# Two scatters in flight instead of four in the routing stage of a four-block kernel

## The chip, the cores and the metric

The kernel runs as one program on one core of one Trainium2 chip. The metric is the device time of one execution in microseconds (us), from the first to the last instruction plus what lies around them; less is better. The kernel before was timed three times.

## What is computed

The reference is four blocks in a row on 8 sequences of 256 tokens of width 256 (2048 tokens), each a residual of a layer norm: attention with 16 heads, a mixture of experts (MoE), a state-space block with 32 heads, and a feed-forward network. The change touches the second:

```
logits = flat @ router_w                       # 2048 tokens, 64 experts
_, topk_idx = top_k(logits + router_bias, 4)
g = silu(einsum('nd,edf->nef', flat, wg));  u = einsum('nd,edf->nef', flat, wu)
routed = einsum('ne,nef,efd->nd', comb, g * u, wd)
shared = two shared experts of hidden width 256 for every token
x = x + layernorm(routed + shared)
```

Only the four chosen experts of a token have a weight in `comb`, so the kernel computes only those.

## The kernel before

One core holds all 2048 tokens as 16 tiles of 128 tokens (`NT = 16`), handled in four chunks of four tiles (`NCH`, `TPC`). The program is a row of stages; each ends in a barrier of all engines. Two stages matter here.

**The routing stage** (`stage_route`). TensorE turns the normalised rows and scores each chunk, VectorE picks the four best experts of each token and works out, for each token and choice, a row number in a table `slots_in` in device memory (128 tiles of 128 rows, each tile owned by one expert). Row numbers of one chunk are ready when `find_slots(g)` has run (the last instruction of it is L1220, semaphore `slots_ready`). VectorE's order is written out by hand: `find_slots(0)`, statistics of x for chunk 2 and 3, `find_slots(1)`, then, when chunks 2 and 3 have been scored, `find_slots(2)`, a step of the shared experts, `find_slots(3)`, and the other shared-expert steps.

GpSimd carries the rows out. For each of the 16 tiles and each of the four choices it issues one indirect DMA (L957, a scatter): the 128 rows of 1 KB of a tile of `rows` go to the 128 row numbers in `slots`. That makes 64 scatters of 128 KB, 16 for each chunk. They use `IN_FLIGHT` semaphores in turn, and scatter n waits until scatter n - `IN_FLIGHT` has landed:

```
if n == BEFORE_ROWS:                                          # 6
    for late in range(EARLY_NORMS, NCH): deviations(OF_X, late)
if n >= IN_FLIGHT:
    pool.wait_ge(scattered[n % IN_FLIGHT], n // IN_FLIGHT * 16)
nc.gpsimd.indirect_dma_start(out=xs[:, :], ...                # L957
    ).then_inc(scattered[n % IN_FLIGHT], 16)
```

A DMA raises its semaphore by 16 when all of it has landed. After the sixth scatter GpSimd computes the deviations and shifts of x for the chunks 2 and 3 (L446, L447). ScalarE needs them to fill `rows` of these chunks (L452), TensorE turns what ScalarE filled (L971), and the scores, the slots and the scatters of these chunks hang on that.

The queue of SyncE issues four loads of expert weights, waits for the semaphores of all scatters, and issues the loads of the first three quads of rows from `slots_in` (`load_quad`, L851).

**The stage behind it** (`stage_slots`) starts after the barrier (L926 is where the routing stage's block closes). TensorE turns quad g (L1359) when its load has landed.

Beside the scatters, TensorE, ScalarE and VectorE compute the shared experts of chunks 0 and 1 (L1032, L1042 on TensorE; L1111, L1115 on ScalarE; L1236, L1240 on VectorE), which ends this stage.

Nothing else waits for single scatters: the semaphores `scattered` are read by GpSimd's own waits and by SyncE alone.

Of the kernel before, what the change touches and what calls it, by code (L numbers as in the profile page):

```python
# [820 lines left out]
COPIES = 3 * QUAD  # L821
DEEP = 3
AHEAD = 4
IN_FLIGHT = 4
WEXP = D + P
U32 = mybir.dt.uint32
I32 = mybir.dt.int32
# [30 lines left out]
def stage_route(chip, x, rows, norms, xh, xl, y, ident, xs, t, ahead, router, ins):  # L858
# [10 lines left out]
    with ExitStack() as ctx:  # L869
# [44 lines left out]
        owner_found, owner_turned, owner_out = (chip.sem(n) for n in ("owner_found", "owner_turned", "owner_out"))  # L914
        slots_ready, scattered = chip.sem("slots_ready"), [chip.kept_sem("scattered") for _ in range(IN_FLIGHT)]
        gate_done, up_done, silu_done = chip.sem("gate_done"), chip.sem("up_done"), chip.sem("silu_done")
# [9 lines left out]
        with nc.Block() as block:  # L926
            @block.sync
            def _(sp):
                for q in range(AHEAD):
                    load_experts(sp, ahead, ins, q, ahead["w_loaded"][q])  # L930
                for done in scattered:
                    sp.wait_ge(done, NT * TOPK // IN_FLIGHT * 16)
                for g in range(DEEP):
# [3 lines left out]
            def _(pool):  # L937
# [3 lines left out]
                def deviations(kind, g):  # L941
                    pool.wait_ge(var_ready, normed(kind, g))
                    spread(nc, link, norms, kind, range(g * TPC, (g + 1) * TPC)).then_inc(rstd_ready, 1)
# [3 lines left out]
                for g in range(NCH):  # L947
                    pool.wait_ge(slots_ready, g + 1)
                    for i in range(g * TPC, (g + 1) * TPC):
                        for k in range(TOPK):  # L950
                            n = i * TOPK + k
                            if n == BEFORE_ROWS:
                                for late in range(EARLY_NORMS, NCH):
                                    deviations(OF_X, late)
                            if n >= IN_FLIGHT:
                                pool.wait_ge(scattered[n % IN_FLIGHT], n // IN_FLIGHT * 16)
                            nc.gpsimd.indirect_dma_start(  # L957
                                out=xs[:, :], out_offset=bass.IndirectOffsetOnAxis(slots[:, i, k:k + 1], 0),
                                in_=rows[:, i, :], in_offset=None).then_inc(scattered[n % IN_FLIGHT], 16)

# [1907 lines left out]
```

## Time and profile before

| | us |
|---|---|
| median of three runs | 1359.48 |
| lowest, highest | 1359.06, 1362.21 |
| the profiled execution, own time | 1354.88 |
| its span, first to last instruction | 1353.1 |
| TensorE busy in it | 1159.4 (86%) |
| VectorE busy | 855.6 (63%) |
| ScalarE busy | 620.5 (46%) |
| GpSimd busy | 362.0 (27%) |
| routing stage, first scatter to its barrier | 258.65 to 372.6 |

The profile is of one execution. The profiled execution's own time lies 4.6 us under the median of the runs, and 1.8 us over its span. Times in the rows are us from the start of the span, durations us unless marked ns. POOL is GpSimd, PE TensorE's matmuls, PEld its weight loads, DVE VectorE, ACT ScalarE, SPq and POOLq the queues of SyncE and GpSimd. A GpSimd row of a scatter is the time in which its descriptors are made, and the transfer comes behind it.

### The profile page before, as it was taken

To read this page: it belongs to the slowest core of one execution; us is meant where nothing else is said; L and a number is where in the kernel's file an instruction comes from. 1 tells how busy PE (TensorE), PEld (TensorE's weight loads), DVE (VectorE), ACT (ScalarE), POOL (GpSimd) and SP (SyncE) were. 2 spreads that over 40 slices of the span, in tenths; PEclk is the share of its full clock that TensorE was granted. 3 is DMA by queue.
4 is the path that set the end of the run, shared out by engine and by line. 5 is a ranking of instruction groups with operands and counts; after the bars stand their busy time and mean duration, and the time that the engine had idled before them with its cause. 6 is when DMAs were issued, how large, how long until landed. Compare 5 with 4: busy or idle time off the path is not lost. (4 is left out here: it accounts for less than half of the span.)

```text
span 1353.1 us, 25314 instructions
## 1 busy us (share of the span) xinstructions
PE 1159.4 (86%) x9088; PEld 966.7 (71%) x9088; DVE 855.6 (63%) x2162; ACT 620.5 (46%) x1420; POOL 362.0 (27%) x460
## 2 busy tenths in 40 slices
PE   6669997347599988677789999999999999999895
PEld 5546775345498977555558888888888888888775
DVE  6467896727566656587365666666666666664474
ACT  5434554112144432467644554554454445553564
POOL 3321231375401437583042014002400240000110
PEclk9779998558899998887899999999999999999898
DMA  6648874121399764253243233223342332221001
GB/s 176 180 120 221 231 204 169 58 101 65 107 360 401 271 246 126 79 183 135 86 119 102 79 102 118 78 79 105 115 140 84 108 107 82 83 86 67 1 17 47
DMA packets 77961, 177.21 MB, mean 131 GB/s; under 512 B 12614, under 2 KB 26182, under 8 KB 75270
## 3 DMA queue, kind: packets, MB, share of 16 engines
q1 hardware_dynamic: 71564, 158.54, 36.2%
q0 software_dynamic: 6272, 17.05, 4.2%
q8 instruction: 73, 1.20, 0.4%
q14 instruction: 52, 0.43, 0.1%
HBM read 114.26 MB, written 61.08 MB: 130 GB/s over the span
## 5 line engine op out<-in xcount | busy, mean ns | idle before, releaser
L2300 ACT ACTIVATE decay<-masked,negcum 128x128 f32<-128x128 f32 x512 | 164.0, 391 | 240.7 <-issue 156.1
L2216 PE MATMUL joint<-xh,w_high 128*128 128x512 f32 x512 | 211.7, 413 | 1.7 <-POOL wl L2157 1.7
L2216 PE MATMUL joint<-xh,wl 128*128 128x512 f32 x512 | 200.6, 392 | 0.0
L2405 DVE COPY cT<-joint 128x512 f32<-128x512 f32 x128 | 88.4, 691 | 176.3 <-PE joint L2216 176.3
L2216 PE MATMUL joint<-xl,w_high 128*128 128x512 f32 x512 | 199.7, 390 | 0.0
L2227 PEld LDWEIGHTS pcb<-cT,bT 128*128 128x128 f32 x1024 | 134.5, 191 | 10.6
L2227 PE MATMUL pcb<-cT,bT 128*128 128x128 f32 x1024 | 135.3, 275 | 0.0
L2154 POOL TENSOR_TENSOR w_high<-w_in,none 128x512 fp32r<-128x512 f32 x32 | 34.6, 1083 | 319.5 <-DMA w_in<-in_w_bc 319.4
L2216 PEld LDWEIGHTS joint<-xh,w_high 128*128 128x128 f32 x512 | 96.5, 188 | 22.5 <-issue 4.8
L2216 PEld LDWEIGHTS joint<-xh,wl 128*128 128x128 f32 x512 | 96.1, 188 | 21.1
L2216 PEld LDWEIGHTS joint<-xl,w_high 128*128 128x128 f32 x512 | 96.6, 189 | 15.3
L2364 DVE TENSOR_TENSOR mixT<-pcb,decay 128x512 f32<-128x512 f32 x128 | 88.5, 692 | 26.2 <-PE pcb L2227 25.9
L2354 DVE TENSOR_TENSOR masked<-cumrow,mask 128x512 f32<-128x512 f32 x128 | 92.2, 721 | 0.0
L697 ACT ACTIVATE probT<-pst 128x384 f32<-128x384 f32 x128 | 60.2, 490 | 65.2 <-PE pst L628 61.8
L2319 ACT ACTIVATE bT<-joint 128x512 f32<-128x512 f32 x128 | 74.3, 581 | 26.3 <-PE joint L2216 26.3
L957 POOL DMA_INDIRECT slots_in<-rows,slots x64 | 65.4, 1023 | 50.5 <-DVE slots L1220 31.8
L1580 POOL DMA_INDIRECT back<-slots_out,slots x64 | 70.2, 1098 | 28.4 <-issue 27.3
L1448 DVE TENSOR_TENSOR rows<-gate,pgu 64x512 f32<-64x512 f32 x64 | 44.2, 691 | 31.2 <-ACT gate L1423 30.8
L1326 POOL COPY copies<-weights 128x384 f32 x64 | 32.4, 507 | 106.3 <-issue 84.7
L2373 DVE TENSOR_TENSOR cS<-cT,grown 128x256 f32<-128x256 f32 x128 | 58.1, 454 | 0.1
L738 DVE CUSTOM_DVE_ANT_0 masked<-ps,reach 128x256 f32<-128x256 f32 x128 | 53.7, 420 | 0.0
L736 DVE CUSTOM_DVE_ANT_0 masked<-ps,reach 128x128 f32<-128x128 f32 x128 | 36.7, 287 | 24.4 <-PE ps L612 23.3
(377 smaller groups left out, 2702.9 us busy)
## 6 DMA issues: line engine op xcount, KB each, us to landing
cumrow<-ssm_cum SPq DMA_DIRECT2D x128, 256.0 KB, 3.3
slots_in<-blank SPq DMA_DIRECT2D x16, 1024.0 KB, 5.4
rows<-slots_in SPq DMA_DIRECT2D x32, 512.0 KB, 5.3
slots_out<-spare SPq DMA_DIRECT2D x32, 512.0 KB, 3.7
weights<-in_expert_quads SPq DMA_DIRECT2D x16, 768.0 KB, 9.2
w_in<-in_w_bc SPq DMA_DIRECT2D x32, 256.0 KB, 3.6
qk_parts<-parts SPq DMA_DIRECT2D x32, 192.0 KB
stack<-qk_parts SPq DMA_DIRECT2D x32, 192.0 KB, 5.3
```

Source lines behind the costliest of these rows:

```text
L697: nc.scalar.activation(probT[:, n % HELD, :], pst[n % T_BANKS][:, 0:3 * P], ACT.Exp).then_inc(exped, 1)
L738: nc.vector.tensor_tensor_reduce(dst[:, P:3 * P], src[:, P:3 * P], reach[:], accum_out=highest[:, u % 2, j, 1:2], **form).then_inc(maxed, 1)
L957: nc.gpsimd.indirect_dma_start(out=xs[:, :], out_offset=bass.IndirectOffsetOnAxis(slots[:, i, k:k + 1], 0), in_=rows[:, i, :], in_offset=N ...
L1580: nc.gpsimd.indirect_dma_start(out=back[:, i % BACK, k, :], out_offset=None, in_=ys[:, :], in_offset=bass.IndirectOffsetOnAxis(slots[:, i, ...
L2216: last = nc.tensor.matmul(bank[:], w[:, j, col:col + P], a[:, k, c * CHUNK:(c + 1) * CHUNK], start=(m == 0), stop=(m == len(parts) - 1))
L2227: last = nc.tensor.matmul(pcb[n % 2][:, o], bT[:, n % 2, o], cT[:, n % 2, o], start=True, stop=True)
L2300: last = nc.scalar.activation(decay[:, n % 2, o], masked[:, n % 2, o], ACT.Exp, bias=negcum[:, c * TPC + i, head:head + 1])
L2319: nc.scalar.activation(bT[:, n % 2, :], pbT[:], ACT.Copy).then_inc(b_out, 1)
L2354: nc.vector.tensor_tensor(masked[:, n % 2, :].rearrange("p (i l) -> p i l", l=P), cumrow[:, n % CUMS, :].rearrange("p (i l) -> p i l", l=P ...
L2364: nc.vector.tensor_tensor(mixT[:, n % KEEP, :], pcb[n % 2][:], decay[:, n % 2, :], ALU.mult).then_inc(mix_out, 1)
L2373: nc.vector.tensor_tensor(cS[:, n % KEEP, :, :], second, grown[:, n % 2, :, :], ALU.mult).then_inc(c_scaled, 1)
L2405: nc.vector.tensor_copy(cT[:, n % 2, :], pcT[:]).then_inc(c_out, 1)
```

## The change

One number changes. `IN_FLIGHT` sets how many semaphores there are, which scatter each scatter waits for, and the count that SyncE waits for on each (64 / `IN_FLIGHT` * 16).

```diff
@@ -821,7 +821,7 @@
 COPIES = 3 * QUAD
 DEEP = 3
 AHEAD = 4
-IN_FLIGHT = 4
+IN_FLIGHT = 2
 WEXP = D + P
 U32 = mybir.dt.uint32
 I32 = mybir.dt.int32
```

No instruction moves on any engine; only waits change. These are GpSimd's first scatters and the deviations behind the sixth, with the waits of each, before the change. A semaphore is shown by the name that first had its number: `qk_whole_55` is `slots_ready` here, and `scattered_18` to `scattered_21` are the four of the ring.

```order
L957 DMA slots_in<-rows,slots_1 16384x256 [waits qk_whole_55]
L957 DMA slots_in<-rows,slots_1 16384x256 x3
L957 DMA slots_in<-rows,slots_1 16384x256 [waits scattered_18]
L957 DMA slots_in<-rows,slots_1 16384x256 [waits scattered_19]
L446 TENSOR_TENSOR norm_rstd<-norm_var,norm_power 128x4 [waits x_in_39]
L447 TENSOR_TENSOR norm_shift<-norm_negmean,norm_rstd 128x4 [waits x_in_38]
```

The same place after the change, with a ring of two.

```order
L957 DMA slots_in<-rows,slots_1 16384x256 [waits qk_whole_55]
L957 DMA slots_in<-rows,slots_1 16384x256
L957 DMA slots_in<-rows,slots_1 16384x256 [waits scattered_18]
L957 DMA slots_in<-rows,slots_1 16384x256 [waits scattered_19]
L957 DMA slots_in<-rows,slots_1 16384x256 [waits scattered_18]
L957 DMA slots_in<-rows,slots_1 16384x256 [waits scattered_19]
L446 TENSOR_TENSOR norm_rstd<-norm_var,norm_power 128x4 [waits x_in_39]
L447 TENSOR_TENSOR norm_shift<-norm_negmean,norm_rstd 128x4 [waits x_in_38]
```

The third to the sixth scatter now wait for the one two places back, where the fifth and sixth waited for the one four places back; so do all 58 behind them.

## Rows read from the trace of the kernel before

**Rows 1.** The page: busy time of each engine, with its share and instructions.

```profile
PE 1159.4 (86%) x9088; PEld 966.7 (71%) x9088; DVE 855.6 (63%) x2162; ACT 620.5 (46%) x1420; POOL 362.0 (27%) x460
```

**Rows 2.** The page, costliest groups: busy, mean ns | idle before, what ended it.

```profile
L957 POOL DMA_INDIRECT slots_in<-rows,slots x64 | 65.4, 1023 | 50.5 <-DVE slots L1220 31.8
```

**Rows 3.** GpSimd in time: start, duration, engine, line, operation [idle before <- released by].

```profile
258.65 1.22 POOL L957 DMA_INDIRECT slots_in<-rows,slots  x1 [18.80 <-DVE slots L1220]
...
261.46 0.96 POOL L957 DMA_INDIRECT slots_in<-rows,slots  x1 [0.30 <-issue]
262.72 0.96 POOL L957 DMA_INDIRECT slots_in<-rows,slots  x1 [0.30 <-issue]
...
265.24 0.96 POOL L957 DMA_INDIRECT slots_in<-rows,slots  x1 [0.30 <-issue]
266.21 1.06 POOL L446 TENSOR_TENSOR norm_rstd<-norm_var,norm_power 128x4 f32<-128x4 f32 x1
```

**Rows 4.** ScalarE and TensorE in time, the first instructions behind the deviations.

```profile
267.61 2.08 ACT L452 ACTIVATE rows<-x,norm_shift,norm_rstd 128x256 f32<-128x256 f32 x4 [25.66 <-POOL norm_shift L447]
...
268.76 1.12 PE L971 MATMUL acc<-ident,rows 128*128 128x128 f32 x4 [19.66 <-ACT rows L452]
```

**Rows 5.** GpSimd in time, from the second chunk's last scatter to the end.

```profile
300.87 0.96 POOL L957 DMA_INDIRECT slots_in<-rows,slots  x1 [0.30 <-issue]
314.80 0.96 POOL L957 DMA_INDIRECT slots_in<-rows,slots  x1 [12.96 <-DVE slots L1220]
...
352.41 0.96 POOL L957 DMA_INDIRECT slots_in<-rows,slots  x1 [0.30 <-issue]
...
357.45 0.96 POOL L957 DMA_INDIRECT slots_in<-rows,slots  x1 [0.30 <-issue]
```

**Rows 6.** Line L926, the stage's closing: queue, operation, duration ns, start.

```profile
L926 POOLq DRAIN  x1: 8865/8865/8865, 354.8 to 354.8; - x1
...
L926 ACTq DRAIN  x1: 1112/1112/1112, 371.4 to 371.4; - x1
```

**Rows 7.** SyncE's queue in time: the three loads behind the last scatter.

```profile
359.94 1.28 SPq L851 DMA_DIRECT2D rows<-slots_in  x3
```

**Rows 8.** Stretches of 0.1 us behind the last scatter: last columns granted clock, DMA share, GB/s.

```profile
358.90:359.00 0.10, 0.00 (x0) 0.00 (x0) 0.00 (x0) 0.00 (x0) 0.00 (x0) 0.50 0.57 205
359.30:359.40 0.10, 0.00 (x0) 0.00 (x0) 0.00 (x0) 0.00 (x0) 0.00 (x0) 0.50 0.25 82
359.50:359.60 0.10, 0.00 (x0) 0.00 (x0) 0.00 (x0) 0.00 (x0) 0.00 (x0) 0.50 0.00 0
```

**Rows 9.** VectorE in time, what released the scatter of 314.80.

```profile
314.35 0.17 DVE L1220 TENSOR_TENSOR slots<-spot 128x16 uint32<-128x16 uint32 x1
```

**Rows 10.** GpSimd in time, gathers of a later stage, the first released inside its gap.

```profile
566.25 1.09 POOL L1580 DMA_INDIRECT back<-slots_out,slots  x1 [0.30 <-DVE y L1857]
567.65 0.95 POOL L1580 DMA_INDIRECT back<-slots_out,slots  x1 [0.30 <-issue]
```

**Rows 11.** Line L851 in 359 to 361.5: landing of the three loads.

```profile
DMA to landing us min/median/max: 3.3/4.2/5.6
```

**Rows 12.** TensorE in time, the first turns of the stage behind.

```profile
372.80 1.07 PE L1359 MATMUL pt<-ident,rows 128*128 128x128 f32 x8 [1.43 <-PEq L926]
374.20 1.10 PE L1359 MATMUL pt<-ident,rows 128*128 128x128 f32 x8 [0.34 <-ACT xT L1413]
...
376.93 1.04 PE L1359 MATMUL pt<-ident,rows 128*128 128x128 f32 x8
```

**Rows 13.** Waits in 225 to 500: us in total, times, longest.

```profile
DVE ranked L1147 <- remote: 18.6, 1, 18.6
ACT gate L1111 <- remote: 8.8, 2, 7.0
DVE prod L1236 <- remote: 7.8, 2, 5.6
```

**Rows 14.** TensorE and VectorE in time, the last score of chunk 3 and its reader.

```profile
285.15 0.40 PE L985 MATMUL pg<-router_wh,xl 128*128 128x64 f32 x1
...
299.33 0.43 DVE L1147 TENSOR_TENSOR ranked<-pg,router_bias 128x256 f32<-128x256 f32 x1 [18.62 <-remote]
```

## The prediction

> **What bounds the kernel now.** I read the page first. TensorE is busy 86% of the span and GpSimd 27% [rows 1], so GpSimd matters only where another engine waits for it. The 64 scatters are 65.4 us of GpSimd's work, and of the 50.5 us idle before them 31.8 us ended with VectorE's slots [rows 2]: this stage is bound by the chain of scores and slots for a good part, not by the scatters. Then the timeline of GpSimd. A scatter takes 0.96 us, and the next starts 0.30 us after its end, so one starts each 1.26 us [rows 3]. Nothing shows a wait of a scatter for a scatter of the ring that costs time; the 0.30 us stands before each of them, waiting or not. Last, the two places at which someone else waits for the scatters: the deviations that follow the sixth [rows 3, 4], and the loads of SyncE and the barrier at the stage's end [rows 6, 7].
>
> **What the change does to one scatter.** Before, scatter n waits for n-4, which started 4 x 1.26 = 5.06 us earlier. After, it waits for n-2, which started 2.53 us earlier and ended 1.56 us earlier (0.30 + 0.96 + 0.30). So the question is one number: how long after its end does a scatter land? Three rows answer.
> - The last scatter starts at 357.45 and ends at 358.41 [rows 5]; SyncE, which waits for all of them, starts its loads at 359.94 [rows 7]. Landing is at most 1.53 us after the end.
> - The transfer behind it is seen at 358.90 and has thinned out at 359.40, with none at 359.50 [rows 8]. Landing is at least 1.0 us after the end.
> - GpSimd's queue reaches the drain behind the last scatter at 354.8, while that scatter starts only at 357.45 [rows 5, 6]. The queue had thus let the last scatter's wait pass at 354.8; that wait is for the scatter four places back, which started at 352.41 and ended at 353.37 [rows 5]. That puts landing at 354.8 - 353.37 = 1.43 us after the end, or 2.4 us after the start.
>
> I take 1.43 us, since it agrees with the other two. It leaves 1.56 - 1.43 = 0.13 us before the scatter that waits would start anyway. So the ring of two is just about filled, and before the change it was never more than two deep either: 2.4 us in flight, one each 1.26 us.
>
> **The price of a wait that ends so late.** In the old order the wait was over 2.65 us before the start; now it is over 0.13 us before it, and how GpSimd behaves there is the unknown. Lower bound: nothing. In a later stage a gather was released inside its gap, still started 0.30 us after the one before, but took 1.09 us in place of 0.95 us [rows 10]; that is +0.14 us for a wait that ends inside the gap. Upper bound: GpSimd starts from idle 314.80 - 314.52 = 0.28 us after VectorE's last slot instruction ended [rows 5, 9]. With the landing at its largest, 1.53 us, the waiting scatter then starts 1.81 us after the end of the one two back instead of 1.56: +0.25 us for a pair, +0.13 us for one. The gather's row is the nearest; a delayed end delays the next two, so I count +0.14 us for a pair, +0.07 us for one. Below nothing is excluded for a single scatter: the change takes no work away and starts none earlier.
>
> **Where that lands on the path.**
> - The head. Scatters 3 to 6 wait now, two pairs, ahead of the deviations at 266.21 [rows 3]. ScalarE had been idle 25.66 us for these and TensorE 19.66 us for ScalarE [rows 4]; nothing covers them. +2 x 0.14 = +0.3 us, between 0 and 0.5. What is queued behind the waiting scatter on GpSimd is the deviations alone.
> - The first half, scatters 7 to 32. Up to 26 x 0.13 = 3.4 us later than 301.83. The next scatter starts at 314.80, having been idle 12.96 us for VectorE [rows 5]. Covered; 0.
> - The second half, 32 scatters. 30 of them with a ring partner in the same half: 30 x 0.07 = 2.1 us later, between 0 and 3.9. SyncE's loads move with the last. They take 3.3 to 5.6 us to land [rows 11], the first at about 359.94 + 3.3 = 363.2, the slowest at 360.8 + 5.6 = 366.4; TensorE first reads a quad at 372.80, held by the barrier, the second at 374.20 and the third at 376.93 [rows 12]. That is 9.6 us of cover for the first and 10.5 for the third. GpSimd's own drain ends at 354.8 + 8.87 = 363.7, and the barrier's last arrival is ScalarE's, at 371.4 + 1.1 = 372.5 [rows 6]: 8.8 us of cover. The shared experts, not the scatters, close this stage. 0 on the path; if the cover were gone, 2.1.
>
> Sum: +0.3 us. The profiled execution becomes 1354.88 + 0.3 = 1355.2 us; it lies 4.6 us under the median of the runs, so on the median 1359.48 + 0.3 = 1359.8 us. The Trainium skill bears on the one number: "DMA: Bandwidth & Descriptors", section "Anatomy of one DMA — SWDGE (gpsimd) path", gives a fixed cost of about 2.0 us for such a DMA plus its bytes at 436 GB/s, mostly spent in the confirmation of the write, which for device memory can be long. For 128 KB that is an estimate of 2.3 us; counted from the start of the scatter it agrees with the 2.4 us of the trace, and counted from the end of the descriptors it would be 0.9 us more and would give the first rival's outcome.
>
> **Rivals.**
> - A. Slower: landing is much later than 1.43 us in some or all of the stretch. The mechanism is the ring itself: a scatter of the second half can't start before the one two back has landed. The shortest landing of a load in this place is 3.3 us from the start [rows 11]; if scatters needed that, a pair would take 3.3 + 0.28 = 3.6 us instead of 2.53, +0.53 us for one. The head pays 4 x 0.53 = 2.1 us, the last 32 pay 17.0 us, of which 8.8 are covered: +8.2. Together +10.3 us, 1369.8. It decides from +0.28 us for a scatter on, where the cover of 8.8 us is used up. Against it: the drain's row and SyncE's start, both under 1.54 us. 8%.
> - B. The stall that the trace doesn't explain. The last matmul of chunk 3's score ends at 285.55 by its row, but VectorE starts to read it at 299.33 [rows 14], released by nothing shown; ScalarE and VectorE have two such waits each later, the longest 7.0 and 5.6 us [rows 13]. All lie beside scatters. If they come of the scatters' pressing on something shared, another pace changes them. Less pressure: the 13.8 us of the first shrink; at most 301.83 to 314.80, 13 us, can be won before the scatters of the first half bound the second; half of it gives -6.5 us, 1353. More of it, by the same half: +6.5 us, 1366. For it: only the place. Against it: the pace changes by a tenth at most in my bounds (0.13 of 1.26 us). 5% faster, 6% slower.
> - C. The change doesn't do what it says: the waits are all over before the scatters would start, and the time is the same to 0.1 us. It can't be told from the forecast by time, only by the trace; it is counted there.
>
> **How the numbers follow.** Forecast with C: 78%. A: 8%. B: 5% and 6%. Something else, about as likely on either side: 3%. A measurement of this kernel tells about 0.3% from no change, which is 4.1 us here: the three runs alone spread over 3.1 us and the profiled execution lies lower still. Of the forecast's 78% I give 2% to each side for that spread. Faster: 2 + 5 + 1 = 8%. Slower: 2 + 8 + 6 + 2 = 18%. Same: 74%. The range: below, the forecast less the spread of the runs, 1359.8 - 3.3 = 1356.5. Above, the upper bound of the head (+0.5), the second half's 3.9 us if its cover were gone, and half the spread of the runs, 1359.5 + 0.5 + 3.9 + 1.6 = 1365.5; most of A and of B lie outside, some 17%.
>
> **What would show it.** Right: in the profile after, scatters start 1.26 to 1.40 us apart with a gap of 0.30 to 0.4 us, some of them released by the DMA; the first to the sixth end at 266.2 to 266.7 if the first starts at 258.65; ScalarE's fill follows at once; the idle before the 33rd scatter is still over 8 us; SyncE's loads start 1.5 us behind the last scatter, and the stage's first turn is still released by the barrier. A shows as gaps of 0.8 us and more and as turns that wait for the load of rows. B shows as unexplained waits of another length with scatters at the old pace. Wrong would be the forecast if GpSimd's restart after a wait that ends late costs far more than 0.28 us, if many single scatters land late, which a ring of four hides and a ring of two does not, or if the deviations take another place in the chain.

## The result, and the profile after

The changed kernel is faster by 1.2%, which was not the forecast: 1342.99 us median of four runs (1339.04 to 1344.0), against 1359.27 us of four runs of the kernel before (1356.89 to 1362.21). The ratio is 0.9876, with a 95% interval of 0.9841 to 0.991. The profiled execution took 1342.61 us (span 1340.8), the one of before 1354.88 (span 1353.1). So 12.3 us are to be found between the two traces.

The page, busy line and the group of the scatters, which answer to [rows 1, 2]:

```profile
PE 1156.2 (86%) x9088; PEld 964.2 (72%) x9088; DVE 854.5 (64%) x2162; ACT 620.4 (46%) x1420; POOL 358.7 (27%) x460
```

```profile
L957 POOL DMA_INDIRECT slots_in<-rows,slots x64 | 63.6, 994 | 45.7 <-DMA slots_in<-rows,slots 19.6
```

No engine does less work. What is new is the releaser: 19.6 of the 45.7 us of idle time before scatters now end with a scatter that landed. GpSimd in time shows how (start, duration, engine, line, operation [idle before <- released by]), to be held against [rows 3]:

```profile
256.12 1.22 POOL L957 DMA_INDIRECT slots_in<-rows,slots  x1 [17.69 <-DVE slots L1220]
257.64 0.99 POOL L957 DMA_INDIRECT slots_in<-rows,slots  x1 [0.30 <-issue]
259.04 0.95 POOL L957 DMA_INDIRECT slots_in<-rows,slots  x1 [0.42 <-DMA slots_in<-rows,slots]
260.33 0.96 POOL L957 DMA_INDIRECT slots_in<-rows,slots  x1 [0.33 <-DMA slots_in<-rows,slots]
...
270.87 0.96 POOL L957 DMA_INDIRECT slots_in<-rows,slots  x1 [0.30 <-issue]
272.27 0.96 POOL L957 DMA_INDIRECT slots_in<-rows,slots  x1 [0.45 <-DMA slots_in<-rows,slots]
273.53 0.96 POOL L957 DMA_INDIRECT slots_in<-rows,slots  x1 [0.30 <-DMA slots_in<-rows,slots]
...
278.86 0.96 POOL L957 DMA_INDIRECT slots_in<-rows,slots  x1 [0.31 <-issue]
282.90 0.96 POOL L957 DMA_INDIRECT slots_in<-rows,slots  x1 [3.07 <-DMA slots_in<-rows,slots]
...
303.23 0.96 POOL L957 DMA_INDIRECT slots_in<-rows,slots  x1 [0.44 <-DMA slots_in<-rows,slots]
304.98 0.96 POOL L957 DMA_INDIRECT slots_in<-rows,slots  x1 [0.80 <-issue]
```

Gaps of 0.30 and 0.42 to 0.45 us alternate, so a pair takes 2.67 us (7.99 us for the three pairs from 270.87 to 278.86) in place of 2.53. One gap is 3.07 us. From the first scatter's start to the 32nd's end it is 48.07 us, against 43.18 before. So far the change costs time.

The gain is where the stall was that the forecast could not explain. TensorE's last score of chunk 3 and VectorE's read of it, which answer to [rows 14]:

```profile
283.04 0.40 PE L985 MATMUL pg<-router_wh,xl 128*128 128x64 f32 x1
...
283.47 0.42 DVE L1147 TENSOR_TENSOR ranked<-pg,router_bias 128x256 f32<-128x256 f32 x1 [4.89 <-PE pg L985]
```

Before, the reader started 13.8 us after the matmul's end, released by nothing shown. Now it starts 0.03 us after it. The slots of chunk 2 are ready at 296.04 in place of 314.52, and the 33rd scatter starts 0.80 us after the 32nd in place of 12.97. The whole stretch from the first scatter to the first turn of the next stage takes 99.7 us in place of 114.2. The closing of the stage, line L926 (queue, operation, duration ns, start), against [rows 6], and the first turn against [rows 12]:

```profile
L926 POOLq DRAIN  x1: 6488/6488/6488, 349.1 to 349.1; - x1
L926 ACTq DRAIN  x1: 1112/1112/1112, 353.8 to 353.8; - x1
...
```

```profile
355.86 1.07 PE L1359 MATMUL pt<-ident,rows 128*128 128x128 f32 x8 [2.08 <-PEq L926]
```

ScalarE arrives at 354.9 and GpSimd at 349.1 + 6.5 = 355.6: the scatters now end the stage, with GpSimd's drain 5.3 us behind the last scatter's end (350.28). Before, ScalarE was 8.8 us later than GpSimd.

The first turn is 16.9 us earlier, of which 2.5 us were there before the first scatter (256.12 against 258.65) and are no work of the change. The whole is only 12.3 us earlier. Of the 4.6 us that are given back, 3.3 are found in stalls of the same unexplained kind beside the gathers of the next stages: behind the barrier, the waits in 355 to 680 that end with "remote" (a releaser that no row shows) add up to 22.0 us before and 25.3 after. Single ones go either way. The two longest (us in total, times, longest), before:

```profile
ACT late_gate L1790 <- remote: 7.5, 1, 7.5
ACT late_hh L1794 <- remote: 7.3, 1, 7.3
```

And after, where `late_gate` is down to 2.2 us:

```profile
ACT late_hh L1794 <- remote: 16.3, 2, 12.3
```

### The profile page after: what moved, and what is told of

Its sections match the earlier page's. It is cut to its first block and busy times, and to the rows that moved or that the text cites. A ratio compares the mean times of both kernels' runs of the same rounds, so it can differ in the third digit from the quotient of the medians.

```text
span 1340.8 us, 25313 instructions
## 1 busy us (share of the span) xinstructions
PE 1156.2 (86%) x9088; PEld 964.2 (72%) x9088; DVE 854.5 (64%) x2162; ACT 620.4 (46%) x1420; POOL 358.7 (27%) x460
## 5 line engine op out<-in xcount | busy, mean ns | idle before, releaser
L957 POOL DMA_INDIRECT slots_in<-rows,slots x64 | 63.6, 994 | 45.7 <-DMA slots_in<-rows,slots 19.6
```

The lines of the kernel that those rows point to most:

```text
L957: nc.gpsimd.indirect_dma_start(out=xs[:, :], out_offset=bass.IndirectOffsetOnAxis(slots[:, i, k:k + 1], 0), in_=rows[:, i, :], in_offset=N ...
```

## Experiments

Each run was timed beside runs of the kernel before on the same chip, and this turned out to matter: the kernel before takes 1360 us on the chip of the prediction and on chip 15, but 1324 to 1327 us on chips 1, 6 and 10. The chip of the prediction has no number on record, and it may be chip 15 itself. Below, "stage" is the time from the first scatter's start to the first turn (L1359) of the next stage in the profiled execution; it is worked out from the same two rows each time.

### The change, again, beside three other rings (chip 1)

Only the number differs: 4, 2, 1, 8.

```diff
-IN_FLIGHT = 4
+IN_FLIGHT = 2    # n2; n3: 1; n4: 8
```

> The kernel before again, unchanged, for its profile on the chip on which the others of this set run. Theory 'stalls of the chip': the waits of VectorE and ScalarE that nothing shown releases (18.6, 7.0 and 5.6 us in the first profile) are a matter of the chip or the time, and are absent here: time near 1324 us, as the kernel before had beside the first four experiments. Theory 'stalls of the program': they are there in every profile of this kernel, near 1359.

> The changed kernel, unchanged, beside the kernel before. If the unexplained waits are absent on this chip for both kernels, the blind sum holds here: +0.3 us in the head, 0 behind it, so a ratio of 0.998 to 1.003. If the change gains by its own mechanism, the ratio is 0.988 again. If the chip has the waits, 0.98 to 1.0 with a shorter first wait in this kernel.

> One scatter in flight: each waits for the one before it. By the landing 1.43 us after the end and a restart 0.14 us behind it a scatter takes 2.5 us instead of 1.26, 64 of them and the deviations about 165 us instead of 100. The cover of the stage's end (some 9 us) is used up and more: the last scatter ends 55 to 65 us later than the one of the kernel before, and the first turn of the next stage waits for its load of rows. 1375 to 1395 us where the kernel before has 1324, 1400 to 1420 where it has 1359. If waits on landings were what removes the unexplained waits, they would be absent here.

> Eight in flight: the waits are over long before. If four never bind, this is the kernel before: ratio 0.998 to 1.002. If the unexplained waits come of scatters pressing, they are as long as with four, where the chip has them at all.

| ring | median, us | ratio to before | 95% interval | stage, us |
|---|---|---|---|---|
| 4 (n1_before) | 1326.58 | 0.9992 | 0.9982 to 1.0003 | 93.95 |
| 2 (n2_after) | 1334.35 | 1.0053 | 1.0034 to 1.0072 | 100.41 |
| 1 (n3_one) | 1416.83 | 1.0663 | 1.064 to 1.0685 | 184.86 |
| 8 (n4_eight) | 1326.94 | 0.9999 | 0.9984 to 1.0014 | 94.06 |

On this chip the same change is slower, by 0.5%, where 0.998 to 1.003 was expected if the waits were absent. What differs most between the chips is the kernel before: it is 33 us faster here, the changed one only 9 us. Here the kernel before has no unexplained wait: the reader of chunk 3's score starts at once, as this row of n1_before shows, where [rows 14] has [18.62 <-remote].

```profile
282.81 0.42 DVE L1147 TENSOR_TENSOR ranked<-pg,router_bias 128x256 f32<-128x256 f32 x1 [4.89 <-PE pg L985]
```

Line L926 of n1_before shows what ends the stage then:

```profile
L926 POOLq DRAIN  x1: 8877/8877/8877, 340.6 to 340.6; - x1
L926 ACTq DRAIN  x1: 1114/1114/1114, 344.7 to 344.7; - x1
```

GpSimd arrives at 349.5 and ScalarE at 345.8. So even before the change the scatters end the stage, by 3.7 us, and every delay of them is paid. Of n2_after, the same line:

```profile
L926 POOLq DRAIN  x1: 6488/6488/6488, 352.9 to 352.9; - x1
```

GpSimd arrives at 359.4, ScalarE at 348.3 + 1.1 = 349.4. With the first scatter at 255.85 and 259.31, the scatters make the stage 6.5 us longer: 4.3 in the first 32 (48.07 against 43.79), 0.5 in the gap behind them (0.79 against 0.31) and 1.7 in the last 32 (45.96 against 44.27).

The waits of scatters in 225 to 500 of n1_before, n2_after and n3_one (us in total, times, longest) tell what the ring does, in this order:

```profile
POOL slots_in L957 <- DMA slots_in<-rows,slots: 0.9, 3, 0.3
```

```profile
POOL slots_in L957 <- DMA slots_in<-rows,slots: 24.0, 50, 2.9
```

```profile
POOL slots_in L957 <- DMA slots_in<-rows,slots: 109.0, 61, 3.2
```

A ring of one measures the disputed number by itself. GpSimd in time, n3_one:

```profile
260.53 0.99 POOL L957 DMA_INDIRECT slots_in<-rows,slots  x1 [1.72 <-DMA slots_in<-rows,slots]
263.23 0.96 POOL L957 DMA_INDIRECT slots_in<-rows,slots  x1 [1.71 <-DMA slots_in<-rows,slots]
265.90 0.96 POOL L957 DMA_INDIRECT slots_in<-rows,slots  x1 [1.71 <-DMA slots_in<-rows,slots]
```

A scatter starts 1.71 us after the end of the one it waits for. With the restart of 0.28 us [rows 5, 9] a scatter lands 1.43 us after its end, as forecast. On this chip the trace has the landings themselves. Of line L957 in n1_before, from the start of a scatter's row:

```profile
DMA to landing us min/median/max: 2.4/2.4/3.3
```

The Trainium skill, "DMA: Bandwidth & Descriptors", section "Anatomy of one DMA — SWDGE (gpsimd) path", gives a fixed cost of about 2.0 us plus the bytes at 436 GB/s, which for 128 KB is an estimate of 2.3 us; counted from the scatter's start, 0.96 + 1.43 = 2.39 us agrees with it, and counted from the end of the descriptors it does not.

The expectation for the ring of one, 1375 to 1395 us, was too low: it took a restart of 0.14 us for the measured 0.28, and all 64 scatters as 165 us in place of 100, where they take 179.3 in place of 88.4. The stage is 90.9 us longer (184.86 against 93.95), which is the whole loss of 90.3 us.

The ring of two has one more cost, which is not regular. These are the long gaps of n2_after in the first half, GpSimd in time:

```profile
285.87 0.96 POOL L957 DMA_INDIRECT slots_in<-rows,slots  x1 [2.86 <-DMA slots_in<-rows,slots]
...
291.41 0.95 POOL L957 DMA_INDIRECT slots_in<-rows,slots  x1 [0.65 <-DMA slots_in<-rows,slots]
...
308.18 0.96 POOL L957 DMA_INDIRECT slots_in<-rows,slots  x1 [0.79 <-DMA slots_in<-rows,slots]
```

A gap of 2.8 to 3.1 us stands once in the first half of after, n2_after, m2_after, m3, r2 and q2_after (2.4 us in e1, 2.0 in p2), and no gap of more than 0.31 us that ends with a scatter stands in n1_before. In each of these traces it lies beside a packet of the instruction queue; the DMA view of after in 279 to 283, around its gap of 3.07 us (queue, kind: packets, MB, share), has one:

```profile
q0 software_dynamic: 96, 0.26, 19.1%
q8 instruction: 1, 0.02, 1.5%
```

That a scatter lands late because of that packet is only argued from the place. That the landing is late, and that a deeper ring hides it, is shown: in the first half the slowest scatter of n2_after and the slowest of n4_eight, with eight in flight, both land 4.3 us after their start where the median is 2.4, and n4_eight has no gap behind it. With three back (m4) such a scatter, of 4.3 us too, leaves one gap of 0.9 us.

### Half of the change at a time, and three places back (chip 10)

Four semaphores are kept, and the wait is taken out of the ring:

```diff
+def places_back(n):
+    return 2 if n < 32 else 4      # e1; e2: 4 if n < 32 else 2; e3: 3; e4: 4
...
-                            if n >= IN_FLIGHT:
-                                pool.wait_ge(scattered[n % IN_FLIGHT], n // IN_FLIGHT * 16)
+                            back = n - places_back(n)
+                            if back >= 0:
+                                pool.wait_ge(scattered[back % IN_FLIGHT], (back // IN_FLIGHT + 1) * 16)
```

The fourth kernel keeps four back, and paces the scatters with a small fill on GpSimd before every second one.

```diff
+                            if n % 2 == 0:
+                                link(nc.gpsimd.memset(filler[:], 0.0))      # 128x256, L966
```

> Only the 32 scatters of chunks 0 and 1 wait two places back; the 32 of chunks 2 and 3 wait four back as before (four semaphores throughout). Theory 'first stall': nearly all of the gain comes of the VectorE wait ahead of the last scores (18.6 us before, 4.9 us after), which lies beside the scatters of chunk 1, so this kernel has it too: 1343 to 1348 us. Theory 'whole stretch' (the slower pace helps all along): half the gain, 1349 to 1353. Theory 'chance' (the stall hangs on the exact moment at which the scatters stand): anything between 1340 and 1360, with the same first half as the changed kernel and so most likely its short wait too.

> The mirror image: chunks 0 and 1 wait four places back as before, chunks 2 and 3 two back. 'First stall': VectorE's wait of 18.6 us stays, 1356 to 1361 us. 'Whole stretch': 1349 to 1353. 'Chance': 1340 to 1360, the first half as before, so most likely the long wait.

> All scatters wait three places back. That wait is over 1.4 us before the scatter can start, so the pace stays one each 1.26 us, as before. If the pace is what matters: 1356 to 1361 us and VectorE's wait of some 18 us. If it matters that GpSimd's queue is held back at all (it may run two scatters ahead instead of three): a part of the gain, 1345 to 1355. If the number of scatters in flight matters, this is as before, since three never are.

> Scatters wait four places back as before, and a memset of 128x256 on GpSimd stands before every second one, so that a pair takes some 0.1 to 0.3 us longer, as in the changed kernel (2.67 us for 2.53), without any wait that ends late. If the pace alone matters: 1340 to 1350 us and the short wait. If the late wait itself matters: 1356 to 1363 and the long one. 'Chance': no rule, any wait between 4 and 19 us.

| kernel | median, us | ratio to before (1323.98) | 95% interval | stage, us |
|---|---|---|---|---|
| e1, two back for the first 32 | 1327.67 | 1.0026 | 1.0004 to 1.0047 | 97.2 |
| e2, two back for the last 32 | 1326.86 | 1.0011 | 0.9993 to 1.0029 | 97.0 |
| e3, three back | 1324.38 | 1.0003 | 0.9983 to 1.0023 | 93.9 |
| e4, four back, paced | 1335.52 | 1.0089 | 1.0059 to 1.0119 | 102.6 |

These were meant to divide a gain, and there was none to divide: this was the first of the chips without the stall. So none of the four times expected for a chip with the stall (1340 us and more) could be tested. What they divide is the cost. Against the 94.0 us of chip 1, since the kernel before has no profile on chip 10, the first half costs 3.1 and the second 2.9 us; together that is 6.0 of the 6.5 us. Three back costs nothing. Pacing alone is dear here: 102.6 us, at 2.83 us for most pairs (2.67 with two in flight), so a slower pace is no gain in itself on such a chip. What these four runs can't say is anything on the gain.

### Is it the number of semaphores? (chip 1 again)

m1 is the kernel before, m2 the changed one, m3 has four semaphores and waits two places back, m4 three places back.

```diff
+def places_back(n):
+    return 2      # m3; m4: 3
```

> The kernel before, unchanged, to see which of two kinds of chip this is. Quiet chip (no unexplained waits): near 1326 us, 94 us from the first scatter to the first turn of the next stage. Chip with stalls: near 1359 us, 114 us, and VectorE's wait of some 18 us ahead of the last scores.

> The changed kernel, unchanged. Quiet chip: 6 to 7 us more than the kernel before, ratio 1.005, 100 us from the first scatter to the turn. Chip with stalls: 12 to 18 us less, ratio 0.988, also 100 us, since the scatters and not the stalls then set the stage's end.

> Every scatter waits two places back, but with four semaphores in turn as before. If only the distance counts, this is the changed kernel: ratio 1.005 on a quiet chip, 0.988 on one with stalls. If the number of semaphores has a part, it lies between it and the kernel before.

> Three places back, the pace of before (one each 1.26 us). Quiet chip: 1.000, 94 us. Chip with stalls: if the stall comes of the pace, as before, 1356 to 1361 us and the 18 us wait; if it hangs on chance timing, it may be short here.

m1 took 1326.78 us, ratio 0.9991 (0.9966 to 1.0015); m2 1336.23, 1.0071 (1.0046 to 1.0097); m3 1336.17, 1.0083 (1.0054 to 1.0112); m4 1327.22, 1.0009 (0.999 to 1.0029). The stages are 94.0, 100.6, 100.6 and 94.1 us. m2 and m3 are the same kernel in all that counts: it is the distance of the wait that costs, not the number of semaphores.

### On a chip that has the stall (chip 15)

q1 is the kernel before and q2 the changed one. p1 and p2 are the same two with 36 idle matmuls (each 128x128, their result read by nobody) on TensorE ahead of chunk 3's score, so that the score comes late in both by the same amount of work.

```diff
+LATER = 36
...
                 turn(3)
+                for _ in range(LATER):
+                    nc.tensor.matmul(pn[:, 3 * P:4 * P], ident[:], ident[:], start=True, stop=True,
+                                     skip_group_check=True)      # L1025
                 score(3)
```

> The kernel before. 1326 us and 94 us of stage on a quiet chip, 1359 and 114 on one with stalls.

> The changed kernel. Quiet chip: 1332 to 1337 us, 100 us of stage. Chip with stalls: about 1343, 100 us of stage, if the first comparison repeats; 1355 and more, with the long wait, if the missing stall was chance.

> Four in flight, and 36 more matmuls of 128x128 f32 (some 0.4 us each, about 14 us) on TensorE ahead of chunk 3's score; their result is not used. On a quiet chip the slots of chunk 2 then come at some 310 us instead of 296, GpSimd is idle for them again, the last scatter ends near 354 and the stage later by 10 to 14 us than without them: 1336 to 1341 us.

> The same late score with two in flight. If the prediction's sum was right for a stage in which the scores come late: the 4.3 us that the first half of the scatters costs vanish in GpSimd's wait, and what is left against the kernel with four is 0 to 2.5 us (head 0.4, second half 2.1 if the scatters still end the stage), where it is 6 to 9 us without the delay. If the distance costs the same whatever the scores do: 6 to 9 us here too.

| kernel | median, us | ratio to before (1360.37) | 95% interval |
|---|---|---|---|
| q1, before | 1359.67 | 1.0 | 0.9978 to 1.0022 |
| q2, after | 1343.13 | 0.987 | 0.9847 to 0.9892 |
| p1, before + 36 matmuls | 1363.83 | 1.0025 | 1.0001 to 1.0048 |
| p2, after + 36 matmuls | 1349.15 | 0.991 | 0.9879 to 0.9941 |

The first result is there again: -16.5 us. VectorE's read of chunk 3's score in q1_before and in q2_after:

```profile
305.42 0.42 DVE L1147 TENSOR_TENSOR ranked<-pg,router_bias 128x256 f32<-128x256 f32 x1 [24.78 <-remote]
```

```profile
285.99 0.42 DVE L1147 TENSOR_TENSOR ranked<-pg,router_bias 128x256 f32<-128x256 f32 x1 [4.89 <-PE pg L985]
```

The stall of 20.2 us behind the matmul's end at 285.20 is gone at this place under the change. It doesn't hang on one exact moment either. With the score put off by the extra matmuls, p2 is still 14.7 us faster than p1, and its reader comes at 299.39 where that of p1 comes at 313.94 (the first scatters start at 258.70 and 257.60). The expectations of p1 and p2 were for a chip without the stall, and aren't tested by these runs.

p1 also shows where its time goes. TensorE in time:

```profile
277.21 5.25 PE L1025 MATMUL counts<-ident 128*128 128x128 f32 x35
282.91 0.37 PE L1025 MATMUL counts<-ident 128*128 128x128 f32 x1 [0.45 <-issue]
284.33 0.27 PE L1025 MATMUL counts<-ident 128*128 128x128 f32 x1 [1.05 <-issue]
285.04 0.36 PE L1025 MATMUL counts<-ident 128*128 128x128 f32 x1 [0.44 <-issue]
286.45 0.37 PE L1025 MATMUL counts<-ident 128*128 128x128 f32 x1 [1.04 <-issue]
...
300.54 0.37 PE L1025 MATMUL counts<-ident 128*128 128x128 f32 x1 [1.74 <-issue]
302.63 0.37 PE L1025 MATMUL counts<-ident 128*128 128x128 f32 x1 [1.72 <-issue]
303.34 5.61 PE L1025 MATMUL counts<-ident 128*128 128x128 f32 x20 [0.33 <-issue]
```

And GpSimd in time, its last scatter of the first half and the first of the second:

```profile
299.84 0.96 POOL L958 DMA_INDIRECT slots_in<-rows,slots  x1 [0.30 <-issue]
326.77 0.96 POOL L958 DMA_INDIRECT slots_in<-rows,slots  x1 [25.97 <-DVE slots L1224]
```

Each of the 36 leaves two records. They wait for no one, and 35 records pass in 5.25 us. Then, from 282.9 to 303.3, there are only 17 in 20.4 us; the rows start at multiples of 0.70 us from each other, each after an idle time that ends with nothing shown. The last 20 pass in 5.61 us from 303.34 on, 2.5 us after the last scatter's end (300.80) and 1.1 us after its landing, if that is 1.43 us behind it. Some explanations don't fit. The granted clock is 1.00 (2.4 GHz) in 283 to 286, where the gaps stand already, and 0.51 in 286 to 300, near the lower level of 1.2 GHz. In p1 the records ahead of the stall are 0.11 us apart at the upper level and 0.21 us at the lower, so the level costs a factor of two, while the rows of the stall stand 0.70 us and more apart. Late instructions are unlikely: from 282.9 to 303.3 the DMA view has packets of scatters alone, and no packet of the instruction queue q8 starts between 275.3 and 318.5, while TensorE is at full pace again from 305 on. Nor did the scatters move more there: the DMA share is 0.30 in 277 to 282, at full pace, and 0.28 in the stall. In p2 the same matmuls run through without a break:

```profile
278.70 10.11 PE L1025 MATMUL counts<-ident 128*128 128x128 f32 x72
```

So in p1, with four in flight, TensorE is held back at issue beside the scatters. That the unexplained wait of VectorE in the kernel before is the same thing is the nearest reading, not shown: there the rows of TensorE show no gap. Scatters alone don't make the stall, since 35 records passed beside them at full pace, and its end isn't theirs everywhere: in the kernel before the reader is released at 299.33, 2.5 us before the 32nd scatter's end. With two in flight TensorE is held less, but p2 still has a wait of VectorE that no row explains, 18.2 us of idle time, of which 8 lie behind the score's last row.

q2's profile shows the same thing from the other side. Its profiled execution took 1355.96 us, 12.8 us over the median of its eight and near the kernel before. The first stall is absent from it, but a later one is there, beside the last scatters of the second half. TensorE in time:

```profile
350.94 0.55 PE L1042 MATMUL acc<-router_sh,hh 128*128 128x256 f32 x1 [8.56 <-issue]
```

Its first turn comes at 372.68, and its stage takes 114.0 us. The stalls are thus fewer or shorter in these traces with two in flight, not abolished, and one execution can lose most of the gain.

### Three back, and two back for the first half, once more (chip 6)

The edits are those of e3 and e1, meant for a chip with the stall.

> Four semaphores, every scatter waits for the one three places back, as in an earlier run on a chip without unexplained waits, where it cost nothing (ratio 1.0003). Open is what it does on a chip that has them (kernel before near 1360). If the stall before the choice of chunk 3 is shortened by scatters that leave less in flight or by waits at their starts, and three back were enough of it, the time falls to some 1343 to 1350, which would make this version as good as two back there and better elsewhere. If the shortening needs the pauses of two back (three back shows none but 0.30 us), the time stays at the kernel before, within 0.3%. On a chip without the stall: within 0.3%, as before, and this run tells nothing new.

> Two places back for the first 32 scatters alone, four back for the rest. On a chip with unexplained waits: if the gain comes from the first half, beside which the 13.8 to 20 us stall of the kernel before lies, it keeps the whole gain and saves 1 to 2 us of the second half, some 1341 to 1345, with VectorE's choice of chunk 3 at about 284 to 286 and the 33rd scatter a few us behind the 32nd at most. If the gain is not from the first half's pace, it stays near 1360. On a chip without the stall: ratio 1.002 to 1.004, as the earlier run of the same edit.

r1 took 1323.74 us, ratio 0.9989 (0.9969 to 1.0008), stage 94.0; r2 1327.92, 1.0022 (0.9999 to 1.0045), stage 97.2. The kernel before took 1324.13 us here: again a chip without the stall. Both repeat e3 and e1 and leave the question open that they were made for.

## Why the prediction was wrong

The step that failed is the one that had no term: the sum left VectorE's wait before chunk 3 [rows 14] as it was and counted only what the scatters lose, +0.3 us. In the result the 13.8 us between the score's end and its reader became 0.03 us, and the stage 14.4 us shorter. Why it did so is open (below).

**Right: the size of one wait.** Landing 1.43 us after a scatter's end is what the ring of one shows (1.71 - 0.28). The price of a wait that ends inside the gap, +0.14 us for a pair, is what the trace of after shows (2.67 against 2.53 us), though as a longer gap (0.42 to 0.45 us for 0.30) and not, as in the gather it was taken from, as a longer row. The head of four waiting scatters, forecast at +0.3 us, took +0.4: from the first scatter's start to the end of the first shift (L447) 9.33 us (after, n2_after) against 8.93 (before, n1_before). The second half, forecast at +2.1 us, took +1.7 (45.30 against 43.61, and 45.96 against 44.27), plus half a microsecond in the gap ahead of it in n2_after. Two slips change nothing: 4 x 1.26 is 5.04 and not 5.06, and the three runs spread over 3.1 us where the range takes 3.3.

**Too small: the first half.** It was bounded at 26 x 0.13 = 3.4 us plus the head's 0.3 and costs 4.9 us in after and 4.3 in n2_after (3.5 to 5.8 in all eight traces with two back there). The regular part is 1.5 to 2 us; the rest is single scatters that land late, 2.5 to 2.7 us of it in one gap. The last paragraph of the prediction names this as a way to be wrong, but no term of the sum priced it. The trace of before could not show it: a ring of four hides it, and that trace has no landings of scatters.

**Wrong as a rule: the cover.** The steps that set 26 and 32 scatters at nothing took 12.96 us of idle time [rows 5] and 8.8 us at the barrier [rows 6] as cover. Both numbers are read rightly, and both hang on the stall [rows 14] and its followers [rows 13]. In n1_before, without the stalls, the first is 0.31 us and the second is below zero: GpSimd is the last at the barrier by 3.7 us. There the forecast +0.3 us would have had to be +6.5 us, and the measured ratios are 1.0053 and 1.0071. Even in the changed kernel of the result GpSimd is last, by 0.7 us (355.6 against 354.9). The forecast held the stall fixed and let the scatters lean on it.

**Wrong in its chances: rival B.** What the result shows is that rival's faster side, the 13.8 us shrink; that less pressure is the reason isn't shown. It was given 5%, with 6% on the slower side and half the stall as its price. In the result all of it went, and the stage became 14.4 us shorter. Two arguments failed. "The pace changes by a tenth at most" looked at the wrong quantity: what changes is also how many scatters are outstanding, and whether GpSimd stands still for 0.15 us in each pair and for 3 us once. And the bound of 13 us looked at the scatters, while ScalarE closed the stage: its arrival at the barrier, counted from the first scatter, came 15.1 us earlier (98.8 against 113.9). Of these, 13.3 come from the reader of chunk 3's score, which starts at 27.35 in place of 40.68. The unexplained waits behind that reader did not go: in this stage they add up to 18.7 us before and 24.7 after. The scatters then end the stage, 0.7 us behind ScalarE.

**Rival A** did not happen as written. Its 3.6 us for a pair is refuted by 2.67, and its mechanism shows only in single scatters. But the scatters do end the stage on the chips without the stall, which this rival had only from +0.28 us for a scatter on.

**Open.** Why TensorE is held back beside scatters in p1, whether the stall of the kernel before is the same, and which part of the change frees it: fewer scatters outstanding, the short pauses, or the one long pause of 3 us, which lies close to the place where the stall would begin (282.9 in p1, the pause of after from 279.8 to 282.9). e1, e3, e4 and m3 would tell these apart on a chip with the stall, and ran on chips without it. Nor is it shown what makes the difference between the chips, beyond that two sets of runs on chip 1 agree (1326.7 and 1326.6 us). So whether three back, which is free on the others, also brings the gain isn't known. Which of two and four is better depends on the chip: two where the kernel before takes 1360 us, four (and three) where it takes 1325.

## What to carry to other kernels

Ask of every idle stretch that is to cover a cost what makes it. If it is made by a wait that no row explains, it is no cover: work out the sum a second time with the wait gone, and give its going a real chance, above all where the change touches what runs beside it. Leave one more transfer in flight than the average landing time asks for, since single late landings decide (here a ring of two fits on paper, and on the chips without the stall three was the first that cost nothing). And measure a change of transfer order on more than one chip before believing its sign.

## What was not expected of the hardware

- The same program takes 1360 us on the chip of the prediction and on chip 15, and 1324 to 1327 us on three others. Some 20 to 24 us of the difference lie in this stage, 114 to 118 us against 94, at the same work.
- On chip 15 TensorE, with nothing to wait for, left 17 records of matmuls in 20.4 us beside the scatters, at multiples of 0.70 us, where it had left 35 in 5.25 us just before.
- The rows of the matmuls may hide this: in the kernel before they show the score finished at 285.55 at full pace [rows 14], while its reader was released at 299.33. The device times of the two kernels go with the reader, not with the row's end, so where the two differ by many us, the reader's start is the safer sign.
- GpSimd's drain behind the last indirect DMA of this stage ends 5.3 us after the last one's end (358.41 to 363.7, 344.22 to 349.5, 350.28 to 355.6). This is longer than the 1.43 us in which the scatter lands, and without the stall, in n1_before, it is what ends the stage.
